# A VectorE step that begins elsewhere, q in four passes, and the low half of k and v on GpSimd

## What is computed

```python
def attn(x, wq, wk, wv, wo):              # head size 64
    Q = einsum('bne,de->bnd', x, wq); K = ...; V = ...
    energy  = einsum('bnd,bne->bde', K, V)            # 64 x 64 per batch
    context = einsum('bnd,bde->bne', Q, energy) * sqrt(3.0 / D)
    return einsum('bnd,ed->bne', context, wo)
def ffn(x, W_fc, W_proj):                 # 256 -> 1024 -> 256
    y = square(relu(x @ W_fc.T)) @ W_proj.T
    # five steps: mem = 0.9 mem + y - (mem > 1);  spike = (mem > 1)
    return spikes.sum(0) / 5
x = x + attn(layernorm(x)); x = x + ffn(layernorm(x))
```

## Time and profile before

| | |
|---|---|
| runs | median 505.34 us of 3 (504.41 to 507.06) |
| the profiled execution, its own time | 501.43 us |
| its span, first to last instruction | 499.5 us |
| mean granted TensorE clock | 0.993 of 2.4 GHz |
| busy: PE, DVE, ACT, POOL | 96%, 69%, 57%, 48% |

### The profile page before, as it was taken

One profiled execution on the slowest core, in us unless ns is written; L12 is line 12 of the kernel. 1 busy time (PEld: TensorE's weight loads), 2 busy tenths in 40 slices (PEclk: granted clock), 3 DMA queues, 4 the chain that ended last, 5 costly groups with the idle time before them and its releaser, 6 DMA issues.

```text
span 499.5 us, 9518 instructions
## 1 busy us (share of the span) xinstructions
PE 478.6 (96%) x3080; PEld 432.7 (87%) x3080; DVE 342.4 (69%) x966; ACT 286.4 (57%) x519; POOL 237.3 (48%) x196
## 2 busy tenths in 40 slices
PE   7899899999999979999999997999999999999995
PEld 6698689899889869898898996898898999999995
DVE  4457658777676776767677855768867674939447
ACT  3427666657566655666566564665746664656540
POOL 1444664473736526374544634545363743535340
PEclk9999999999999999999999998999999999999998
DMA  8413021130403113040312212131110101010102
GB/s 310 99 44 69 17 42 44 54 75 36 93 0 85 43 55 73 0 126 0 85 42 64 63 43 42 43 79 47 55 30 0 42 2 42 1 43 1 44 1 84
DMA packets 60705, 26.46 MB, mean 53 GB/s; under 512 B 55552, under 2 KB 56192, under 8 KB 60416
## 3 DMA queue, kind: packets, MB, share of 16 engines
q1 hardware_dynamic: 60672, 26.09, 19.1%
HBM read 17.69 MB, written 8.39 MB: 52 GB/s over the span
## 4 chain that ended last, share of the span: by engine, by line
PE 79%; DVE 10%; issue 6%; ACT 2%; DMA 1%; POOL 1%; SPq 0%; DVEq 0%; POOLq 0%
PE hid_ps L814 10%; PE hid_ps L815 10%; PE hid_ps L816 10%; PE y_ps L816 10%; PE y_ps L815 10%; PE y_ps L814 10%; PE work_ps L856 3%; PE y_ps L823 2%; DVE stat L592 2%; PE work_ps L922 2%; DVE cnt L701 2%; PE work_ps L923 2%; DVE cnt L720 1%; PE kv_ps L814 1%; PE kv_ps L815 1%
## 5 line engine op out<-in xcount | busy, mean ns | idle before, releaser
L355 POOL TENSOR_TENSOR hid_l<-hid,hid_h 128x512 fp32r<-128x512 f32 x128 | 165.2, 1296 | 204.7 <-ACT hid_h L409 204.5
L398 ACT ACTIVATE relu<-hid_ps 128x512 f32<-128x512 f32 x128 | 76.6, 598 | 112.1 <-PE hid_ps L816 110.6
L815 PE MATMUL y_ps<-wdn_l,hid_h 128*128 128x256 f32 x480 | 136.1, 284 | 0.0
L816 PE MATMUL y_ps<-wdn_h,hid_l 128*128 128x256 f32 x480 | 136.1, 283 | 0.0
L814 PE MATMUL y_ps<-wdn_h,hid_h 128*128 128x256 f32 x480 | 135.7, 283 | 0.0
L814 PE MATMUL hid_ps<-x2T_h,wup_h 128*128 128x512 f32 x256 | 105.5, 412 | 0.5 <-ACT relu L398 0.3
L815 PE MATMUL hid_ps<-x2T_l,wup_h 128*128 128x512 f32 x256 | 100.9, 394 | 0.0
L816 PE MATMUL hid_ps<-x2T_h,wup_l 128*128 128x512 f32 x256 | 100.3, 392 | 0.0
L814 PEld LDWEIGHTS y_ps<-wdn_h,hid_h 128*128 128x128 f32 x480 | 92.0, 192 | 5.1
L815 PEld LDWEIGHTS y_ps<-wdn_l,hid_h 128*128 128x128 f32 x480 | 92.0, 192 | 4.9
L816 PEld LDWEIGHTS y_ps<-wdn_h,hid_l 128*128 128x128 f32 x480 | 91.9, 192 | 0.0
(11 more groups left out here) (125 smaller groups left out, 611.7 us busy)
## 6 DMA issues: line engine op xcount, KB each, us to landing
xs<-x_dram SPq DMA_DIRECT2D x15, 512.0 KB, 3.3
out_dram<-x SPq DMA_DIRECT2D x15, 512.0 KB, 2.7
x_block<-x_dram SPq DMA_DIRECT2D x104, 64.0 KB, 2.5
hid<-w_up_dram SPq DMA_DIRECT2D x1, 1024.0 KB, 8.1
x<-w_down_dram SPq DMA_DIRECT2D x1, 1024.0 KB, 10.2
xs<-x_dram SPq DMA_DIRECT2D x2, 256.0 KB, 2.8
out_dram<-x SPq DMA_DIRECT2D x1, 256.0 KB, 2.0
out_dram<-x SPq DMA_DIRECT2D x2, 128.0 KB, 1.9
```

What stands on the lines that cost most here:

```text
L355: nc.gpsimd.tensor_tensor(hid_l[:, i % 2, c, :], hid[:, c % 4, :], hid_h[:, i % 2, c, :].bitcast(f32), ALU.subtract).then_inc(hid_ready, 1)
L398: nc.scalar.activation(relu[:, c % 2, :], hid_ps[c % 2][:, :], ACT.Relu).then_inc(relu_done, 1)
L815: mm(dst, a[0], b[1], start=False, stop=False)
L816: return mm(dst, a[1], b[0], start=False, stop=stop)
```

## The change

- **Where VectorE's step begins.** The 12 operations of `spikes` on the second y bank move from the end of step i - 1 to step i, six at its head and six behind the energy sum; `first_moments(i+3)` moves behind `eo_low_half`. GpSimd's matching `inverse_deviation(i+3, 0)` moves from before chunk 1 to before chunk 4.
- **Loops.** FIRST is 2: the loop has two iterations, which begin at steps 2 and 6; steps 10 to 16 are straight.
- **q in four passes.** The stationary operand wq_hl is [high | low] of wq, 64 columns each. Times xT_h it gives both high by high (partitions 0 to 63) and low by high (64 to 127); two passes of wq high times xT_l add to partitions 0 to 63. q is then the sum of the two halves of the bank: `q_high_half` rounds the first, and `q_low_half` is two VectorE operations, a remainder into kv_scaled and the sum with the second half.
- **k and v.** In all steps but step 0, `kv_low_half` runs on GpSimd, at the end of its step.
- **The start.** The `keep_warm` rounds 8, 4, 2, 16, 4 become 3, 2, 2, 12, 4, and ScalarE's and VectorE's work is reordered.

The diff, cut (names of semaphores wqq_* become wq_*):

```diff
-FIRST = 1
+FIRST = 2
...
@@ GpSimd
+            def kv_low_half(r, n):
+                pool.wait_ge(kv_high, upto(r, n + 1))
+                src = kv_scaled[:, :].rearrange("p (a d) -> p a d", d=HEAD)
+                high = kv[:, :, :, 0, :].rearrange("p t s d -> p (t s) d")
+                low = kv[:, :, :, 1, :].rearrange("p t s d -> p (t s) d")
+                nc.gpsimd.tensor_tensor(low, src, high.bitcast(f32), ALU.subtract).then_inc(kv_ready, 1)
...
-                    if c == 1 and there(r, i + 3):
+                    if c == (1 if is_first(r, i) else 4) and there(r, i + 3):
                         inverse_deviation(r, 2 if is_first(r, i) else i + 3, 0)
...
                 if is_first(r, i):
                     inverse_deviation(r, 3, 0)
+                elif there(r, i + 3):
+                    kv_low_half(r, i + 3)
@@ ScalarE
-                nc.scalar.activation(qT[:, n % 2, :], q_bank(r, n)[:, :], ACT.Copy).then_inc(q_high, 1)
+                nc.scalar.activation(qT[0:HEAD, n % 2, :], q_bank(r, n)[0:HEAD, :], ACT.Copy).then_inc(q_high, 1)
...
+            half_of_columns(w_loaded["up"], wup_raw, wup_h, wup_high, 0)
             kvT_out(0, 0)
+            q_high_half(0, 0)
+            half_of_columns(w_loaded["up"], wup_raw, wup_h, wup_high, 1)
+            kvT_out(0, 1)
             kv_high_half(0, 0)
-            half_of_columns(w_loaded["up"], wup_raw, wup_h, wup_high, 0)
-            q_high_half(0, 0)
-            kvT_out(0, 1)
+            q_high_half(0, 1)
             kv_high_half(0, 1)
-            half_of_columns(w_loaded["up"], wup_raw, wup_h, wup_high, 1)
+            half_of_columns(w_loaded["down"], wdn_raw, wdn_h, wdn_high, 0)
             energy_first_half(0, PER_BATCH - 1)
-            q_high_half(0, 1)
+            half_of_columns(w_loaded["down"], wdn_raw, wdn_h, wdn_high, 1)
             eo_high_half(0, PER_BATCH - 1)
...
@@ VectorE
+                if not isinstance(r, int) or n >= 2:
+                    dve.wait_ge(q_ready, 3 if isinstance(r, int) and n == 2 else upto(r, n))   # in kv_scale
...
             def q_low_half(r, n):
                 dve.wait_ge(q_high, upto(r, n + 1))
-                nc.vector.tensor_tensor(qT[HEAD:P, n % 2, :], q_bank(r, n)[HEAD:P, :],
-                                        as_f32(qT[HEAD:P, n % 2, :]), ALU.subtract).then_inc(q_ready, 1)
+                dve.wait_ge(kv_ready, 2 if isinstance(r, int) and n < 3 else upto(r, n + 1))
+                if there(r, n - 1):
+                    dve.wait_ge(q_ready, upto(r, n))
+                nc.vector.tensor_tensor(kv_scaled[HEAD:P, :], q_bank(r, n)[0:HEAD, :],
+                                        as_f32(qT[0:HEAD, n % 2, :]), ALU.subtract).then_inc(q_rest, 1)
+                dve.wait_ge(q_rest, upto(r, n + 1))
+                nc.vector.tensor_tensor(qT[HEAD:P, n % 2, :], q_bank(r, n)[HEAD:P, :], kv_scaled[HEAD:P, :], ALU.add)\
+                    .then_inc(q_ready, 1)
...
+                if there(r, i - 2):
+                    spikes(r, i - 2, 1, range(0, PAIR_OPS // 2))
                 if there(r, i + 3):
                     turn_blocks(r, i + 3)
-                    first_moments(r, i + 3)
                 if there(r, i + 2):
                     q_low_half(r, i + 2)
                 if there(r, i + 2) and closes_batch(i + 2):
                     energy_sum(r, i + 2)
+                if there(r, i - 2):
+                    spikes(r, i - 2, 1, range(PAIR_OPS // 2, PAIR_OPS))
                 if there(r, i + 2) and closes_batch(i + 2):
                     eo_low_half(r, i + 2)
+                if there(r, i + 3):
+                    first_moments(r, i + 3)
                 if there(r, i + 1):
                     residual(r, i + 1)
...
                     kv_scale(r, i + 3)
-                    kv_low_half(r, i + 3)
-                if there(r, i - 1):
-                    spikes(r, i - 1, 1, range(PAIR_OPS))
...
@@ VectorE, the start
             xT_low_half(0, 0)
-            low_half_of_weights(wqq_high, wqq_raw[:, :], wqq_h, wqq_l, wqq_ready)
+            dve.wait_ge(wq_high, 1)
+            nc.vector.tensor_tensor(wq_hl[:, :, 1, :], ..., ALU.subtract).then_inc(wq_ready, 1)
+            xT_low_half(0, 1)
             first_moments(0, 1)
-            xT_low_half(0, 1)
             kv_scale(0, 0)
             kv_low_half(0, 0)
-            q_low_half(0, 0)
             kv_scale(0, 1)
             kv_low_half(0, 1)
+            q_low_half(0, 0)
             energy_sum(0, PER_BATCH - 1)
             q_low_half(0, 1)
@@ TensorE
+                both = [wq_hl[:, k, :, :].rearrange("p s d -> p (s d)") for k in range(EC)]
+                mm(q_bank(r, n)[:, :], both[0], xT_h[:, n % 2, 0, :], start=True, stop=False)
                 for k in range(EC):
-                    last = three(q_bank(r, n)[:, :], (wqq_h[:, k, :], wqq_l[:, k, :]),
-                                 (xT_h[:, n % 2, k, :], xT_l[:, n % 2, k, :]), k == 0, k == EC - 1)
+                    mm(q_bank(r, n)[0:HEAD, :], wq_hl[:, k, 0, :], xT_l[:, n % 2, k, :], start=False, stop=False)
+                last = mm(q_bank(r, n)[:, :], both[1], xT_h[:, n % 2, 1, :], start=False, stop=True)
...
-            keep_warm(8)
+            keep_warm(3)
...
-            keep_warm(4)
+            keep_warm(2)
...
-            keep_warm(16)
+            keep_warm(12)
```

More of the change, by code:

```diff
@@ L91, in build @@
         wkv_h, wkv_l = (sb(f"wkv_{s}", [P, EC, 2 * HEAD], f32r) for s in "hl")
-        wqq_h, wqq_l = (sb(f"wqq_{s}", [P, EC, 2 * HEAD], f32r) for s in "hl")
+        wq_hl = sb("wq_hl", [P, EC, 2, HEAD], f32r)
         wup_h, wup_l = (sb(f"wup_{s}", [P, EC, HID], f32r) for s in "hl")
@@ L174, in build @@
         averager_ready, mean_done = sem("averager_ready"), sem("mean_done")
-        wkv_centred, wqq_centred = sem("wkv_centred"), sem("wqq_centred")
+        wkv_centred, wq_centred = sem("wkv_centred"), sem("wq_centred")
         wkv_high, wkv_ready = sem("wkv_high"), sem("wkv_ready")
-        wqq_high, wqq_ready = sem("wqq_high"), sem("wqq_ready")
+        wq_high, wq_ready = sem("wq_high"), sem("wq_ready")
         wup_high, wup_ready = sem("wup_high"), sem("wup_ready")
@@ L188, in build @@
         kv_turned, kv_in_scale, kv_high, kv_ready = sem("kv_turned"), sem("kv_in_scale"), sem("kv_high"), sem("kv_ready")
-        q_done, q_high, q_ready = sem("q_done"), sem("q_high"), sem("q_ready")
+        q_done, q_high, q_rest, q_ready = sem("q_done"), sem("q_high"), sem("q_rest"), sem("q_ready")
         energy_done, energy_out, energy_ready = sem("energy_done"), sem("energy_out"), sem("energy_ready")
@@ L519, in _ @@
             high_half_of_weights(wkv_centred, wkv_raw[:, :], wkv_h, wkv_high)
-            high_half_of_weights(wqq_centred, wqq_raw[:, :], wqq_h, wqq_high)
+            act.wait_ge(wq_centred, 1)
+            nc.scalar.activation(wq_hl[:, :, 0, :], wqq_raw.rearrange("p (k s n) -> p k s n", k=EC, s=2)[:, :, 0, :], ACT.Copy).then_inc(wq_high, 1)
             xT_high_half(0, 0)
             xT_high_half(0, 1)
+            half_of_columns(w_loaded["up"], wup_raw, wup_h, wup_high, 0)
             kvT_out(0, 0)
+            q_high_half(0, 0)
+            half_of_columns(w_loaded["up"], wup_raw, wup_h, wup_high, 1)
+            kvT_out(0, 1)
             kv_high_half(0, 0)
-            half_of_columns(w_loaded["up"], wup_raw, wup_h, wup_high, 0)
-            q_high_half(0, 0)
-            kvT_out(0, 1)
+            q_high_half(0, 1)
             kv_high_half(0, 1)
-            half_of_columns(w_loaded["up"], wup_raw, wup_h, wup_high, 1)
+            half_of_columns(w_loaded["down"], wdn_raw, wdn_h, wdn_high, 0)
             energy_first_half(0, PER_BATCH - 1)
-            q_high_half(0, 1)
+            half_of_columns(w_loaded["down"], wdn_raw, wdn_h, wdn_high, 1)
             eo_high_half(0, PER_BATCH - 1)
-            half_of_columns(w_loaded["down"], wdn_raw, wdn_h, wdn_high, 0)
-            half_of_columns(w_loaded["down"], wdn_raw, wdn_h, wdn_high, 1)
             x2T_high_half(0, 0)
@@ L779, in step @@
                     kv_scale(r, i + 3)
-                    kv_low_half(r, i + 3)
-                if there(r, i - 1):
-                    spikes(r, i - 1, 1, range(PAIR_OPS))
             centre_weights(w_loaded["kv"], wkv_raw[:, :], 0, wkv_centred)
-            centre_weights(w_loaded["qq"], wqq_raw[:, :], 1, wqq_centred)
+            centre_weights(w_loaded["qq"], wqq_raw[:, :], 1, wq_centred)
             first_moments(0, 0)
@@ L789, in _ @@
             xT_low_half(0, 0)
-            low_half_of_weights(wqq_high, wqq_raw[:, :], wqq_h, wqq_l, wqq_ready)
+            dve.wait_ge(wq_high, 1)
+            nc.vector.tensor_tensor(wq_hl[:, :, 1, :], wqq_raw.rearrange("p (k s n) -> p k s n", k=EC, s=2)[:, :, 0, :], as_f32(wq_hl[:, :, 0, :]),
+                                    ALU.subtract).then_inc(wq_ready, 1)
+            xT_low_half(0, 1)
             first_moments(0, 1)
-            xT_low_half(0, 1)
             kv_scale(0, 0)
```

(10 more changed lines are left out.)

## The result

| | before | after |
|---|---|---|
| runs | median 504.99 us of 4 (504.41 to 507.06) | median 483.9 us of 4 (483.19 to 484.44) |
| ratio | | 0.957, 95% interval 0.954 to 0.961 |
| profiled execution, its time | 501.43 us | 484.38 us |
| its span, mean granted clock | 499.5 us, 0.993 | 482.4 us, 0.991 |

The forecast was 485.4, in a range of 481 to 493. The page's busy line of the changed kernel answers to the earlier trace rows: TensorE 11 us less, VectorE and GpSimd more.

A forecast was written before the change was run, and what follows sets the result against it. TensorE, busy 96% of the span, was taken as the bound. Against the profiled 501.43 us, -7.4 - 1.5 - 6.0 - 3.6 + 0.5 = -18.0 gave 483.4; keeping about half of the median's 3.9 excess made 485.4, range 481 to 493.

The forecast's parts named there:

- q in four passes: TensorE's q matmuls: two fewer save 0.46 us in each of 13 steps, -6.0 us.
- step 0: In step 0, bound by VectorE, the second q operation adds 0.7 us, of which 0.5 shows: +0.5 us.
- The start: Before step 0: fewer transposes and the new order give -4.2 us, or -3.6 with kv_low_half lengthened.
- waits for the energy sum, and the clock behind one: TensorE's six waits in closing steps go, -7.4 us, and the clock no longer falls behind one, -1.5 us.
- The energy sum, earlier: VectorE's new order in closing steps ends the energy sum at T+7.9; TensorE wants it at T+10.05; T is chunk 0's start.
- Who pays: VectorE's later work in a step: idle time before a closing step's residual falls from 3.02 to 0.7 us, costed at nothing.
- the rival that gave it nothing: 64-column passes or changing tile shapes cost TensorE what two q passes saved: 491.4 us, chance 0.10.
- GpSimd's kv_low_half: In the steps, moved off VectorE: takes 1.3 us, ends by T+3.5, and takes 1.02 us from VectorE's work.
- the clock falls behind TensorE's waits: Rival for the start: fewer transposes leave TensorE idle and the clock falls, 1.5 us each: 489 us, chance 0.08.
- The contention: In the start, VectorE's two kv_low_half lengthen beside GpSimd's subtractions: +0.3 us twice.
- The median: Runs of before stood 3.9 us above the profiled execution; about half was kept, moving 483.4 to 485.4.

The follow-up runs named there:

- the six-pass run: The changed kernel with q in six matmuls and one VectorE operation, as in the kernel before: 489.66 us.
- GpSimd later: The changed kernel with GpSimd splitting w_up and w_down only after both kv_low_half of the start: 482.41 us.

## Why the prediction was right, point by point

Against the profiled executions, in us:

| term | forecast | measured | from |
|---|---|---|---|
| start | -3.6 | -1.1 | first up projection 37.62 to 36.54 |
| step 0 | +0.5 | +0.5 | second half of `turn_second` 56.38 to 55.78, less the start |
| waits for the energy sum, and the clock behind one | -8.9 | -8.9 | none left; 7.4 of idle time, and step 9 1.5 longer than step 5 |
| q, 13 steps | -6.0 | -6.0 | 0.46 a step |
| what each of the six waits cost beyond its idle time | none | -1.6 | below |
| sum | -18.0 | -17.1 | 499.5 to 482.4 |

From the second half of `turn_second` in step 0 (56.38 and 55.78) to `turn_second` in step 13 (431.34 and 414.25) it is 374.96 us before and 358.47 now. The last three terms add up to these 16.5.

- **The energy sum, earlier:** right in its mechanism and, within 0.2 us, in its times: q_low T+6.05 for T+6.2, the energy sum T+7.8 for 7.9, TensorE's call for it T+9.9 for 10.05, 0.61 us before the residual for 0.7. What I left out is that a wait costs TensorE more than its idle time. In the closing steps with a wait of 0.40 it is 29.09 us from one `turn_second` to the next (112.08 to 141.17 in the trace of before) and 27.97 now; 0.40 and 0.46 explain 0.86 of 1.12. The other 0.26, six times, are the 1.6 of the table, and the lines of that wait show where they lie.

```profile
126.34 0.28 PE L816 MATMUL y_ps<-wdn_h,hid_l 128*128 128x256 f32 x1
127.02 0.70 PE L912 MATMUL e_ps<-wo,energy 128*128 128x256 f32 x2 [0.40 <-DVE energy L667]
127.36 0.58 PE L814 MATMUL hid_ps<-x2T_h,wup_h 128*128 128x512 f32 x1
```

Idle time is counted from the end of the last record, 0.28 us after its start, but without a wait the next matmul starts 0.12 us after it: 0.68 here instead of 0.12. That is 0.16 of the 0.26; the other 0.09 is that L814 starts 0.34 us after L912, and 0.25 now (179.43 to 179.68). The same slip made TensorE's call 0.17 us late in the forecast.

- **Where the wait came from:** I had read the loop's iteration head as part of it. The run with FIRST = 2 shows that it was what made the two waits long, and half of the gain; the new order makes the place of the head indifferent (FIRST = 3 costs nothing). That the gap would stand in steps 2 and 6 was wrong: in the changed kernel it stands nowhere.
- **Who pays:** nobody, as forecast. normalise lengthened from 1.97 to 2.34 us, which I had not foreseen; it still ends 1.5 us before `turn_second`.
- **q in four passes:** right, and the rival that gave it nothing is out. One argument against that rival was misread: matmuls of 512 and 256 columns do follow at 0.23 and 0.12 us, but the four of 128 columns of the energy take 0.10 each (176.17 to 176.57), not a quarter of 0.23. Its worth hangs on the other parts: alone it lengthens VectorE's queue, which was the bound in the closing steps.
- **GpSimd's kv_low_half:** I had counted it as what takes 1.0 us off VectorE; it was hardly needed (0.7 us between medians, with overlapping runs, 0.34 of it where the loop's gap fell). ScalarE's half of the energy sets when the sum can start.
- **The start:** the step that failed; it was put at -3.6 us and gave -1.1. Two costs were wrong.
  - *The clock.* I named the rival (the clock falls behind TensorE's waits) and gave it 0.08; it happened. The waits were 1.54 and 2.11 us where I had reckoned 0.8 and 1.7. With them filled, step 0 begins 0.5 to 1.6 us earlier.
  - *The contention.* I took the steps' 1.02 us of the earlier trace rows as the price beside GpSimd, and beside the larger w_up split it was 1.66 and 1.25. The rule of the Trainium skill (GPSIMD Engine Reference, Key points) that I had set beside it names VectorE instructions with two SBUF inputs, and also those in a 2-port perf mode, which I had left out. The traces agree on the first kind: kv_low_half takes 0.69 us both times once GpSimd waits, and the spike operations beside the moved one keep their 0.35. But an operation of one large SBUF operand lengthened as well: normalise takes 1.38 us with GpSimd idle and 3.38 beside its subtractions in step 0. No run shows in which mode it runs.
  - With both mended and w_down moved, step 0 begins at 34.14, 3.5 us before 37.62, so what was missing of the start's 3.6 lies in these costs.
  - But 37.62 is no firm base. 1.0 us of it is a late x, which the same code did not have in the run with FIRST = 2 (36.61). In the changed kernel x came as late (TensorE waited 0.98 us) without a cost, as its 12 transposes ended when xT_l did. Against 36.61 the first trace of the changed kernel (36.54) gains 0.1 us and the second (35.42) 1.2.
- **The median:** I kept 2.0 of the 3.9 us by which the runs of before stood above its profiled execution. None stayed: 483.9 against 484.38. They were falls of the clock behind the waits that the change removes: with FIRST = 2 alone, no wait over 0.41 us is left in the steps, the clock falls nowhere in the trace, and four executions lie within 0.08 us. So the forecast of 485.4 is near in part by luck, as errors of both signs met: +2.5 in the start, -1.6 for the waits' further cost, -2.0 kept for the clock, and -0.5 because the profiled execution of the changed kernel was one of its longer ones.

## What to carry to other kernels

Where the bounding engine waits for one small operation of another, move what is not urgent behind that operation before shortening anything; saving work on the bounding engine first, at the price of one more operation on the other, made this kernel slower. See what a loop's iteration head falls on: a gap of 2.5 us there made a wait of 0.40 us into one of 2.99 where VectorE was late already, and cost nothing where it had slack. Price a wait of TensorE from start to start of its matmuls, not by its idle time. Price the clock behind it as a chance: here some waits of 1.5 us and more were followed by a fall and some were not. And read the clocks of the timed runs and the start of more than one trace, not only those of one profiled execution.

## What the runs showed of the hardware

- The idle time of "issue" on VectorE came only where an iteration begins that follows another, never at the first, and there not always: 2.5 us in steps 5 and 9 of the kernel before; with FIRST = 2 never in the changed kernel or in before's order, but 2.45 us in step 6 of the six-pass run and 2.17 with kv_low_half on VectorE; with FIRST = 3 2.42 us in step 7. What decides it stays open.
- In the start the clock fell with waits of 1.54 and 2.11 us (the changed kernel) and of 0.57 and 1.55 (GpSimd later), but not in the traced execution of the six-pass run with 0.27 and 2.10, nor in before with 0.59 and 1.77. In the steps it fell behind one wait of 2.97 us but not behind another of 2.99 in the same execution, and behind both of 4.16 and 4.13.
- Transposes of the identity put into the waits kept the granted clock at 1.00 from 16 to 28 us, where it was 0.50 for 3.4 and 6.8 us in the two traces without them.
- A 64-column stationary operand changed nothing in the pitch of its 512-column matmuls, 0.23 us, and neither did changing between it and the 128-column ones.
- VectorE's subtraction of two SBUF operands, 0.69 us alone, took 1.02 us beside GpSimd's subtractions of its own size and up to 1.68 beside those of twice the size. GpSimd's two subtractions of w_up, in turn, took 5.14 us instead of 4.69.
